# A gated attention and expert kernel on one core: the order of the work in its head, and the division of the last output sums

## The reference

```python
# cross-attention: latent = layernorm(x), batch = context
weights = softmax((latent @ Wq.T) @ (context @ Wk.T).T / sqrt(128))
x = x + tanh(g_xattn) * (weights @ (context @ Wv.T))
# expert block on layernorm(x), 16 experts
logits = unit(x) @ unit(sim_matrix) - sigmoid(gates)     # top-2 fallback where no logit is positive
w = softmax of relu(logits) over the chosen experts      # [token, 16]
q, k, v = sum over e of w[:, e] * (x @ proj[e])          # three projections, 16 experts each
o = softmax(q @ k.T / sqrt(128)) @ v                     # inside each sequence of 128 tokens
out = sum over e of w[:, e] * (o @ o_proj[e])            # 16 experts again
x = x + tanh(g_ffn) * out
```

## Time and profile before

| | |
|---|---|
| median of 3 runs | 841.78 us (841.29 to 841.8) |
| the profiled execution | 841.99 us |
| its span, first to last instruction | 839.9 us |
| TensorE busy | 796.5 us (95%) |
| VectorE busy | 583.7 us (69%) |
| GpSimd busy | 481.0 us (57%) |
| ScalarE busy | 434.2 us (52%) |
| granted TensorE clock, mean | 0.997 |

### The profile page before, as it was taken

The page is one execution under the profiler, slowest core; times in us unless marked ns, Lnnn a source line. Parts: engine busy times, 40 slices in busy tenths (PEclk is TensorE's granted clock), DMA queues, the critical chain, the costliest instruction groups (busy, mean ns, idle before and its releaser), DMA issues.

```text
span 839.9 us, 13842 instructions
## 1 busy us (share of the span) xinstructions
PE 796.5 (95%) x4111; PEld 431.5 (51%) x4111; DVE 583.7 (69%) x1993; ACT 434.2 (52%) x1134; POOL 481.0 (57%) x702
## 2 busy tenths in 40 slices
PE   5579999999999999999999999999999999999995
PEld 4345555555555555555555555555555555544442
DVE  3767676768587676758767675876767586676647
ACT  4555646455454645545464554546455454543433
POOL 3265656564665656466665646666564665655524
PEclk9999999999999999999999999999999999999998
DMA  6373453534444333444333434443244443325100
GB/s 188 98 240 120 153 183 115 154 132 131 140 145 128 112 117 131 122 140 151 126 121 95 143 121 140 151 124 129 72 149 131 140 150 117 113 59 184 65 9 25
DMA packets 71099, 106.40 MB, mean 127 GB/s; under 512 B 6960, under 2 KB 45552, under 8 KB 71024
## 3 DMA queue, kind: packets, MB, share of 16 engines
q1 hardware_dynamic: 70304, 105.44, 40.1%
q10 hardware_dynamic: 720, 0.08, 0.1%
HBM read 89.51 MB, written 15.99 MB: 126 GB/s over the span
## 4 chain that ended last, share of the span: by engine, by line
PE 74%; DVE 14%; DMA 4%; issue 3%; ACT 3%; POOL 1%; SPq 1%; DVEq 0%; ACTq 0%; POOLq 0%
PE acc_q L1176 16%; PE acc_k L1176 16%; PE acc_v L1176 16%; PE y L1188 7%; PE oT_p L1188 7%; DVE x_all L986 4%; DVE zq_full L957 2%; PE oT_p L1379 2%; DVE logit L906 2%; PE m L1248 2%; PE m L1303 1%; PE m L1289 1%; ACT y_sc L625 1%; PE m L1239 1%; DMA stage<-in_L_ffn_k_proj_dram 1%
## 5 line engine op out<-in xcount | busy, mean ns | idle before, releaser
L538 POOL TENSOR_TENSOR zq<-zq_full,zq 128x512 f16<-128x512 f32 x256 | 294.9, 1161 | 298.7 <-ACT zq L612 297.5
L612 ACT ACTIVATE zq<-zq_full 128x512 f16<-128x512 f32 x256 | 160.8, 640 | 246.2 <-DVE zq_full L957 243.7
L1176 PE MATMUL acc_q<-zq,w_hi 128*128 128x512 f16 x512 | 194.6, 380 | 2.8 <-POOL zq L538 2.8
L1176 PE MATMUL acc_k<-zq,w_hi 128*128 128x512 f16 x512 | 194.5, 380 | 0.0
L1176 PE MATMUL acc_v<-zq,w_hi 128*128 128x512 f16 x512 | 194.5, 380 | 0.0
L986 DVE SCALAR_TENSOR_TENSOR x_all<-y,w_out,x_all 128x128 f32<-128x128 f32 x356 | 121.8, 342 | 80.1 <-issue 71.2
L957 DVE TENSOR_TENSOR zq_full<-wq_bc,x2T_p 128x512 f32<-128x512 f32 x256 | 167.4, 672 | 3.3 <-DMA wq_bc<-w_rows 2.5
L986 DVE SCALAR_TENSOR_TENSOR x_all<-oT_p,w_out,x_all 128x128 f32<-128x128 f32 x356 | 121.3, 341 | 0.0
L552 POOL TENSOR_TENSOR x_all<-y_sc,x_all 128x128 f32<-128x128 f32 x240 | 100.3, 454 | 20.1 <-DVE x_all L986 13.3
L1176 PE MATMUL acc_q<-zq,w_lo 128*128 128x512 f16 x256 | 97.3, 380 | 0.0
L1176 PE MATMUL acc_v<-zq,w_lo 128*128 128x512 f16 x256 | 97.3, 380 | 0.0
(11 more groups left out here) (191 smaller groups left out, 1110.0 us busy)
## 6 DMA issues: line engine op xcount, KB each, us to landing
wq_bc<-w_rows SPq DMA_DIRECT2D x128, 512.0 KB, 4.4
out_dram<-x_all SPq DMA_DIRECT2D x16, 256.0 KB, 6.8
blk_rows<-v_blk SPq DMA_DIRECT2D x15, 256.0 KB, 4.2
v_mix<-blk_rows SPq DMA_DIRECT2D x60, 64.0 KB, 2.0
blk_rows<-pc_blk SPq DMA_DIRECT2D x15, 256.0 KB, 3.3
pcT<-blk_rows SPq DMA_DIRECT2D x60, 64.0 KB, 2.0
blk_rows<-xn_blk SPq DMA_DIRECT2D x13, 256.0 KB, 2.6
xn_mix<-blk_rows SPq DMA_DIRECT2D x52, 64.0 KB, 3.4
```

The source lines that it names most:

```text
L538: nc.gpsimd.tensor_tensor(zq[:, 1, e % Z_SLOTS, :], zq_full[:, e % F_SLOTS, :], zq[:, 0, e % Z_SLOTS, :], ALU.subtract).then_inc(zq_lo_poo ...
L612: nc.scalar.activation(zq[:, 0, e % Z_SLOTS, :], zq_full[:, e % F_SLOTS, :], ACT.Copy).then_inc(zq_hi_done, 1)
L1176: last = nc.tensor.matmul(acc[m][:], w[:, m, s, :], zq[:, half, s % Z_SLOTS, :], start=(s == 0 and n == 0), stop=(s == E - 1 and n == 2))
```

## The change

Order of the head:

- VectorE: `setup_gate` moves ahead of `share_largest`, `first_stats(1)` ahead of `weight_scales(0)`; V's low half moves behind the products of experts 0 and 1; the statistics of group 1 come ahead of the product of expert 3.
- ScalarE: wT is copied, and x2T moved, ahead of K's high half; V's high half moves behind `pxT_out(1)`.
- GpSimd: `second_rstd(1)` moves from the start of pass 0 to between the low halves of z for experts 2 and 3.
- Each weight has a semaphore of its own for its high and its low half. TensorE does the first expert in a new order (`first_expert`): for Q, K and V the products with z's high half, each when its weight half is there; then the three with z's low half.

End:

- The table says how many of a pair's two banks VectorE takes (2, 1 or 0). In the last group pair 5 is now (2, 2) with one bank for each side, pair 6 is (3, 0), so GpSimd adds 4 blocks more there. All other groups divide as before.
- The last group is stored in two parts, its first two sequences when pair 6 is added.

```diff
-Y_PAIRS_LAST = ((0, 0, True), (0, 2, False), (1, 0, True), (1, 2, False),
-                (2, 0, True), (3, 0, True), (2, 2, True), (3, 2, True))
+Y_PAIRS_LAST = ((0, 0, 2), (0, 2, 0), (1, 0, 2), (1, 2, 0), (2, 0, 2), (2, 2, 1), (3, 0, 2), (3, 2, 2))
...
+            def store_last():
+
+                wait(sp, y_added, added(NG - 1, PAIRS_Y - 1))
+                sp.dma_start(o_v[:, B - 4:B - 2, :], x_all[:, B - 4:B - 2, :]).then_inc(out_stored, 16)
+                wait(sp, y_added, added(NG - 1, PAIRS_Y) + 1)
+                sp.dma_start(o_v[:, B - 2:B, :], x_all[:, B - 2:B, :]).then_inc(out_stored, 16)
...
# GpSimd
-                for e in range(LEAD):
+                for e in range(LEAD - 1):
                     zq_low(0, e)
+                second_rstd(1)
+                zq_low(0, LEAD - 1)
                 first_rstd(2)
...
-                    for b in range(2):
-                        wait(pool, y_pool_added, ADDS * n + 2 * j + b - 1)
+                    for b in range(first, 2):
+                        wait(pool, y_pool_added, done - (1 - first))
...
# ScalarE
-                weight_high(K)
-                wT_out(0)
-                weight_high(V)
-                x2T_move(0)
+                wT_out(0)
+                x2T_move(0)
+                weight_high(K)
                 x_exps(1)
                 vx_out(1)
                 pxT_out(1)
+                weight_high(V)
...
                         y_scale(gc, 1)
                         y_scale(gc, 3)
+                        y_scale(gc, 5, banks=(1,))
...
# VectorE
                 weight_max(V)
+                setup_gate()
                 share_largest(0)
+                first_stats(1)
                 weight_scales(0)
-                setup_gate()
-                first_stats(1)
...
                 weight_low(K)
-                weight_low(V)
                 x_sum(1)
                 zq_scale(0, 0)
                 zq_scale(0, 1)
+                weight_low(V)
+                zq_scale(0, 2)
                 x1_add(1)
-                zq_scale(0, 2)
+                second_stats(1)
                 zq_scale(0, 3)
-                second_stats(1)
                 first_stats(2)
...
# TensorE
+            def first_expert():
+
+                pe.wait_ge(share_step, 3)
+                pe.wait_ge(xnT_sb, 2)
+                pe.wait_ge(zq_hi_done, 1)
+                for m in (Q, K, V):
+                    pe.wait_ge(hi_done[m], 1)
+                    nc.tensor.matmul(acc[m][:], w_hi[:, m, 0, :], zq[:, 0, 0, :], start=True, stop=False)
+                    pe.wait_ge(lo_done[m], 1)
+                    nc.tensor.matmul(acc[m][:], w_lo[:, m, 0, :], zq[:, 0, 0, :], start=False, stop=False)
+                wait_zq_low(pe, 0, 0)
+                for m in (Q, K, V):
+                    last = nc.tensor.matmul(acc[m][:], w_hi[:, m, 0, :], zq[:, 1, 0, :], start=False, stop=False)
+                last.then_inc(zq_used, 1)
```

More of the change, by code:

```diff
@@ L198, in flamingo_gated_moe_attention @@
         wmax_ps = sem("wmax_ps")
-        hi_done = sem("hi_done")
-        lo_done = sem("lo_done")
+        hi_done = [sem(f"hi_done{m}") for m in range(4)]
+        lo_done = [sem(f"lo_done{m}") for m in range(4)]
         nrm_root = sem("nrm_root")
@@ L318, in on_dve, with added, scaled @@
         def on_dve(g, p):
[L319 to L327, removed]
+            return y_pairs(g)[p][2] > 0
+        def added(g, p):
+            return QUAD * (12 * g + sum(pair[2] for pair in y_pairs(g)[:p]))
+        def scaled(g, p):
+            return 4 * g + sum(2 - pair[2] for pair in y_pairs(g)[:p])
         def wait_y_read(eng, g, p):
[L331 to L334, removed]
+            if y_pairs(g)[p][2] > 0:
+                wait(eng, y_added, added(g, p + 1))
+            if y_pairs(g)[p][2] < 2:
+                wait(eng, y_scaled, scaled(g, p + 1))
         def wait_y_summed(eng, g, p):
@@ L342, in wait_y_summed @@
             elif on_dve(g, same[-1]):
-                wait(eng, y_added, ADDS * (dve_pairs(g, same[-1]) + 1))
+                wait(eng, y_added, added(g, same[-1] + 1))
             else:
-                wait(eng, y_pool_added, ADDS * (pool_pairs(g, same[-1]) + 1))
+                wait(eng, y_pool_added, QUAD * scaled(g, same[-1] + 1))
         def wait_zq_low(eng, g, e):
@@ L419, in store @@
             def store(g):
[L420 to L421 removed]
+                wait(sp, y_added, added(g + 1, 0))
+                wait(sp, y_pool_added, QUAD * scaled(g + 1, 0))
                 sp.dma_start(o_v[:, bass.ds(G * g, G), :], x_all[:, bass.ds(G * g, G), :]).then_inc(out_stored, 16)
+            def store_last():
[3 more added lines that the diff above has]
+                sp.dma_start(o_v[:, B - 2:B, :], x_all[:, B - 2:B, :]).then_inc(out_stored, 16)
             def head():
@@ L478, in body @@
                         spread_q(g2, 3)
-                    if s == 11 and has(gd):
+                    if s == 11 and has(gd) and gd < NG - 1:
                         store(gd)
@@ L541, in y_pool_add @@
             def y_pool_add(g, p):
-                k, b0, _ = y_pairs(g)[p]
-                n = pool_pairs(g, p)
-                wait(pool, y_scaled, 2 * n + 2)
+                _, b0, first = y_pairs(g)[p]
+                n = scaled(g, p)
+                wait(pool, y_scaled, scaled(g, p + 1))
                 if g < NG - 1:
                     wait_y_summed(pool, g, p)
+                done = QUAD * n
                 for j in range(QUAD):
-                    for b in range(2):
-                        wait(pool, y_pool_added, ADDS * n + 2 * j + b - 1)
+                    for b in range(first, 2):
+                        wait(pool, y_pool_added, done - (1 - first))
                         total = rows(x_all, g, b0 + b) if g < NG - 1 else y_rest[:, b, :]
-                        nc.gpsimd.tensor_tensor(total, y_sc[:, n % 2, b, j, :], total,
+                        nc.gpsimd.tensor_tensor(total, y_sc[:, n // 2 % 2, b, j, :], total,
                                                 ALU.add).then_inc(y_pool_added, 1)
+                        done += 1
             def head():
@@ L567, in body @@
                 for s in range(E):
-                    if s == 0 and has(g2):
+                    if s == 0 and i > 0 and has(g2):
                         second_rstd(g2)
@@ L613, in zq_high, with y_scale @@
                                      ACT.Copy).then_inc(zq_hi_done, 1)
-            def y_scale(g, p):
+            def y_scale(g, p, banks=(1, 0)):
                 k, b0, _ = y_pairs(g)[p]
-                n = pool_pairs(g, p)
+                n = scaled(g, p)
                 wait(act, w_out_done, 2 * g + 2)
                 wait(act, y_ps, PAIRS_Y * g + p + 1)
-                wait(act, y_pool_added, ADDS * (n - 1))
-                for b, bank in ((1, y_banks(g, p)[1]), (0, y_banks(g, p)[0])):
+                wait(act, y_pool_added, QUAD * (n - 2))
+                for b in banks:
+                    bank = y_banks(g, p)[b]
                     for j in range(QUAD):
                         e = QUAD * k + j
-                        last = nc.scalar.activation(y_sc[:, n % 2, b, j, :], bank[:, tok(j)], ACT.Copy,
+                        last = nc.scalar.activation(y_sc[:, n // 2 % 2, b, j, :], bank[:, tok(j)], ACT.Copy,
                                                     scale=w_out[:, g % 2, e, b0 + b:b0 + b + 1])
@@ L982, in y_add @@
                 for j in range(QUAD):
-                    for b, bank in enumerate(y_banks(g, p)):
+                    for b, bank in enumerate(banks):
                         e = QUAD * k + j
-                        wait(dve, y_added, n - 1)
+                        wait(dve, y_added, n - len(banks) + 1)
                         nc.vector.scalar_tensor_tensor(
@@ L1339, in body @@
                 for s in range(E):
-                    if has(i):
+                    if (i, s) == (0, 0):
+                        first_expert()
+                    elif has(i):
                         experts(i, s)
@@ L1376, in body @@
                         elif gc > 0:
-                            wait(pe, y_scaled, 2 * pool_pairs(gd, PAIRS_Y - 1) + 1)
+                            wait(pe, y_scaled, scaled(gd, PAIRS_Y - 1) + 1)
                         for b in range(G):
```

32 lines of the change are left out of this document (15 added, 17 removed).

## The result

The changed kernel takes 836.51 us (836.07 to 836.82, 6 runs) against 841.65 (840.91 to 842.15, 6 runs) on the same chip: ratio 0.9939, 95% interval 0.9926 to 0.9952. The forecast was 838.7 with a range from 837.1: right in sign, too small by 2.2 us. The profiled execution took 836.16 us, its span 834.4. The page and the stage table first: the work (but for four sums that moved from VectorE to GpSimd) and the middle stretch are the same.

A forecast was written before the change was run, and what follows sets the result against it. TensorE, busy 95% of the span, bounds the kernel, so only its stalls in head and end were for sale: 1.9 (head) + 1.0 + 0.2 (end) = 3.1 us, giving 838.7; own range 837.9 to 839.4, with rivals 837.1 to 840.7.

The forecast's parts named there:

- Step 1: Head, VectorE: setup_gate ahead of the scales; logits and gate chain start 1.34 us earlier.
- Step 2: Head, ScalarE: wT's copy ahead of K's high half, 2.92 us earlier together with Step 1; first product at 43.65.
- Step 3: Head, TensorE: first expert by high halves, starting at 45.1 in place of 49.32.
- Step 4: Head: V's low half in VectorE's queue collides with GpSimd, whose first subtraction ends about 48.3, not 46.2.
- GpSimd comes first: Rival, 20%: in the head VectorE's queue slips by 1.1 us; head gains 1.2, total 2.4, time 839.4.
- no collision: Rival, 12%: no collision in the head and an undisturbed gate; head gains 2.9 to 3.7, time 836.9 to 837.7.
- Where the head then hangs: Head, queues from GpSimd's subtractions to the gate: wmax_d at 66.8 to 67.2, 1.9 us for the head.
- The head's upper bound, 3.7: Most the head could gain: 3.7 us, set by TensorE's own arrival at the wait on wmax_d, 65.2 against 68.91.
- Steps 5 and 6: End: half a pair to GpSimd, closing add 1.0 us earlier; two stores, the half-size last one saving 0.2.
- The slower rival: Rival, 5%: TensorE's clock stays low in the head; 842.2 through expert 3, about 848 up to wmax_d.

The follow-up runs named there:

- sn_only: The kernel before with one edit: setup_gate ahead of share_largest and group 1's statistics ahead of the scales; 839.88 us, 0.9981.
- wT_late: The changed kernel with the copies of wT and x2T put back behind K's high half on ScalarE; 838.73 us, 0.997.
- first_old: The changed kernel with TensorE's first expert in the old form, waiting for all low halves, then nine matmuls; 836.4 us, 0.9943.
- v_quarters: The changed kernel with V's low half in four pieces of 4 experts, three of them behind products 5 and 7; 836.89 us, 0.9948.
- one_store: The changed kernel with the last four sequences stored by one transfer again, behind the closing add; 836.92 us, 0.9945.
- wT_only: The kernel before with one edit: on ScalarE wT's copy and x2T's move ahead of K's high half; 841.37 us, 0.9998.
- rstd_old: The changed kernel with second_rstd(1) on GpSimd back at the start of pass 0, behind first_rstd(2); 840.7 us, 0.9988.
- share_late: The changed kernel with TensorE's spread_max(1) and VectorE's weight_scales(1) one step later in pass 0; 836.64 us, 0.9949.

## Why the prediction was too low

The marks of the head, as forecast and as measured:

| mark | forecast | measured | earlier by |
|---|---|---|---|
| row store issued | 36.0 | 35.82 | 0.18 |
| first broadcast | 39.3 | 38.18 | 1.12 |
| first product | 43.65 | 42.47 | 1.18 |
| `second_rstd(1)` ends | 52.55 | 51.26 | 1.29 |
| x2's transposes | 55.4 | 54.16 | 1.24 |
| group 1's gate | 61.6 | 60.17 | 1.43 |
| `wmax_d` (its transposes) | 67.0 | 65.19 | 1.8 |

**Step 1 was right.** The logits start 1.47 earlier (1.34 forecast), the gate chain 1.50, and 0.19 of either stands ahead of the change. `sn_only` is worth 1.9 us by itself; in its profile the first product comes 2.18 earlier, of which 0.38 stands ahead of its edit and 0.40 is a first broadcast that took 3.95 us to its product instead of 4.35.

**Step 2 is where the sum failed.** ScalarE's copy came 3.15 earlier (2.92 forecast), but the row store behind it was carried over at its old 3.29 us. It took 2.36, so the first product came 4.12 earlier, not 2.94. That mis-sized term, 0.93 us, is half of the head's shortfall of 1.82; of the rest 0.18 stands at the store's issue (the profiles' own 0.19), 0.06 at the first product, 0.25 at the gate and about 0.4 behind it. All five profiles with wT's copy behind K's high half (four kernels and the kernel before once more) have the 16 KB fetch in the store, the 8 KB one ahead of it, and 2.96 to 3.45 us. All nine with it ahead have the 8 KB fetch in the store, the 16 KB one only after 46 us, and 2.09 to 2.36. That the order of ScalarE's queue decides is shown by `wT_late`, one swap; that it does so by the fetch, and which engine's instructions these are, is argued from the pairing and was not tested by itself.

**Step 3 was right in time and worth nothing.** TensorE starts at 44.08 (45.1 forecast) and breaks for 0.29 before z's low half (0.7 foreseen); `first_old` shows that its whole gain falls into slack.

**Step 4 was right.** The first subtraction ran 3.1 us beside V's low half (43.90 to 47.0, TensorE released at 47.09), and it was GpSimd that was held: VectorE's low half took its usual 2.34 us. "GpSimd comes first" and "no collision" are both refuted. The total came out below even the range of the second, for other reasons. VectorE's low half had begun first, by 0.23 us here and by 1.14 at O's. Where the subtraction had begun first it was VectorE that was held: in `v_quarters` a quarter begun inside a subtraction took 1.11 us, one begun ahead of it 0.75. So far as these rows go, the one that begins later waits.

```profile
43.12 0.75 DVE L900 SCALAR_TENSOR_TENSOR w_lo<-stage,w_up,w_hi 128x512 f16<-128x512 f32 x1
...
49.67 1.11 DVE L900 SCALAR_TENSOR_TENSOR w_lo<-stage,w_up,w_hi 128x512 f16<-128x512 f32 x1
```

```profile
43.34 3.77 POOL L543 TENSOR_TENSOR zq<-zq_full,zq 128x512 f16<-128x512 f32 x3 [13.87 <-ACT zq L623]
...
49.07 1.16 POOL L543 TENSOR_TENSOR zq<-zq_full,zq 128x512 f16<-128x512 f32 x1
```

The Trainium skill's sentence on the shared interfaces (GPSIMD Engine Reference, Key points) holds here in direction; the factor, 3.1 for 1.16, is these rows'.

**"Where the head then hangs"** had the right chain (`second_rstd`, x2, logits, norm, gate), with 0.25 too much up to the gate. Behind the gate it allowed 5.2 to 5.6 us; from the gate to the transposes it took 5.02 where it was 5.67, about 0.4 less than allowed: of the collisions with subtractions one fell out whole (an operation of 0.88 us at 63.50, right behind the gate's first, takes 0.23 after), one shrank (0.94 at 66.43 to 0.53) and a new one came (0.58 at 61.59 in place of 0.16), 0.64 in all, where the prediction allowed one "of up to 0.7". And the prediction priced nothing for pass 1, though the trace of the kernel before has a wait on a transfer there; 0.37 went in this pair of profiles, and by the other profiles this term is anything from 0 to 1.03, whatever the change. The head's upper bound, 3.7, was met for another reason than the one it was built on: TensorE arrived at 63.95, not at 65.2, and still waited 1.24.

**Steps 5 and 6 were right:** 1.01 for 1.0, 0.39 for 0.2 (0.42 to the tail of `one_store`). The section of the Trainium skill by which the prediction estimated 0.3 (DMA: Bandwidth & Descriptors, Anatomy of one DMA) gives its figures for transfers that GpSimd issues; here SP issues, and the traces decide. The twenty adds end at 831.55, 0.13 ahead of the closing add, and VectorE's last add at 831.57: both finish together.

**The slower rival** did not come true in the change (1.20 us of idle before x2's transposes, 0.66 for them), but its mechanism did in `wT_only`, `rstd_old` and `share_late`. As far as the traces of `wT_only` and `rstd_old` show, it is why the parts don't add: wT alone 0.4 (within its error of nothing), `sn` alone 1.9, and the whole head 3.3, all of which is lost again with `second_rstd` at its old place. One of the readings it was built on was wrong: in the 10 us before the first expert TensorE had worked for 4.9, not for most of them.

## What to carry to other kernels

Where several queues converge on one point, cost the parts together: here moving the weights forward gained nothing that can be told unless the statistics that the next transpose waits for move too, and the idle stretch opened between them costs the clock as well. A transfer's length from the old order is a term with its own error; look at what else ran in its window (an instruction fetch, another queue) before carrying it over. And once the engine arrives before its data, a further microsecond saved upstream need not reach the end: in `v_quarters` it was gone again after a wait on a transfer and two longer passes.

## What was not expected of the hardware

- A 32 KB store beside a 16 KB instruction fetch took 2.96 to 3.45 us from issue to the next transfer's issue, beside one of 8 KB 2.09 to 2.36 (five and nine profiles).
- Idle of TensorE before the same four transposes, and their length: 1.04, 1.20, 1.56 and 1.90 us with 0.66; 1.91 us (`share_late`) with 0.73 and the next expert at the lower clock; 2.53 with 1.08; 4.39 with 1.12. The mean granted clock of a whole run (0.991 to 0.999) doesn't tell them apart; that of the stretch does: 0.50 from 57 to 62 us in `rstd_old` and from 58 to 60 in `wT_only`, 0.57 from 54 to 58 in `share_late`. Not always: in the kernel before it reads 1.00 from 49.3 to 53.1, where the matmuls start 0.427 us apart, so their spacing is the safer sign.
- A last store of half the size shortened the tail by 0.42 us (2.72 to 2.30). The table of transfers gives 2.3 us for 128 KB and for 256 KB alike, but that is a median over two stores: the first of 128 KB landed in 2.8 us and the last, which ends the span, in 1.8.
- The same kernel's wait on one transfer in pass 1 was 0.37 us in one profile and 1.03 in another; in three others with the same pass 1 it was nothing. The first broadcast took 3.95 to 4.44 us to its product wherever VectorE was free for it. Two profiles' marks can differ by as much without any change of the kernel.
